# Relative attention: position tables inside the layernorm ahead, steps split last, first batch split by two engines

## What is computed

```python
Q, K, V = heads(x @ Wq.T + bq), heads(x @ Wk.T + bk), heads(x @ Wv.T + bv)   # 16 heads of 8
pos_key   = (rel_emb @ Wpk.T + bpk).reshape(128, 16, 8)
pos_query = (rel_emb @ Wpq.T + bpq).reshape(128, 16, 8)
scores = Q K^T * scale
scores += take(Q pos_key^T, clip(j - i + 64, 0, 127)) * scale
scores += take(K pos_query^T, clip(i - j + 64, 0, 127))^T * scale
out = softmax(scores) V @ Wo.T + bo
```

## Time and profile before

| what | us |
|---|---|
| median of three runs | 2801.14 (2800.57 to 2802.79) |
| the profiled execution | 2805.52 |
| its span | 2803.7 |
| TensorE busy | 2424.5 (86%) |
| VectorE busy | 2077.3 (74%) |
| ScalarE busy | 1585.5 (57%) |
| GpSimd busy | 269.5 (10%) |
| the layernorm ahead of the layer begins | 1457.0 |
| the layer's first instructions | 1471.1 |
| first band product | 1498.3 |
| first score product | 1519.1 |
| the next layernorm begins | 2026.4 |

### The profile page before, as it was taken

How to read it: one execution, slowest core, us unless ns; L and a number is a source line. 1 busy time by engine, 2 the same in 40 slices (tenths; PEclk the granted TensorE clock), 3 DMA queues, 4 the chain that set the end, 5 groups by cost and what they waited for, 6 DMA issues and landing times. The chain is left out here.

```text
span 2803.7 us, 64145 instructions
## 1 busy us (share of the span) xinstructions
PE 2424.5 (86%) x25861; PEld 1600.8 (57%) x25861; DVE 2077.3 (74%) x3811; ACT 1585.5 (57%) x4086; POOL 269.5 (10%) x278
## 2 busy tenths in 40 slices
PE   6888888888888888888994999999998887999777
PEld 5666676666666676674442666666642332332376
DVE  6899898899999989892124777788727775886465
ACT  3566666666667666665334777777641113667344
POOL 0000000000000000000011101100003342110342
PEclk9999999999999999999996999999999998999889
DMA  5111111110111111002007998999510003220421
GB/s 188 32 33 25 25 32 33 32 32 18 32 32 33 33 32 32 17 17 72 0 12 198 229 250 227 229 244 236 130 37 2 0 0 108 70 74 20 176 70 65
DMA packets 205727, 219.50 MB, mean 78 GB/s; under 512 B 32966, under 2 KB 191446, under 8 KB 199990
## 3 DMA queue, kind: packets, MB, share of 16 engines
q1 hardware_dynamic: 202400, 209.59, 28.5%
q0 software_dynamic: 2400, 4.95, 0.5%
q10 hardware_dynamic: 633, 0.85, 0.1%
HBM read 137.96 MB, written 79.79 MB: 78 GB/s over the span
## 5 line engine op out<-in xcount | busy, mean ns | idle before, releaser
L3003 DVE TENSOR_REDUCE dl_ZO<-dl_XP 128x64 f32<-128x128 f32 (+6 forms) x448 | 219.7, 491 | 15.4
L2116 ACT ACTIVATE da_AB<-ps 128x384 f32<-128x384 f32 x256 | 124.7, 491 | 137.7 <-PE ps L1963 134.1
L2578 PE MATMUL ps<-dl_ST,ident 128*128 128x512 f32 x416 | 187.8, 595 | 0.0
L2998 DVE TENSOR_TENSOR dl_XP<-dl_ZO,dl_G 128x128 f32<-128x128 f32 (+5 forms) x384 | 177.1, 461 | 13.2
L1596 DVE TENSOR_REDUCE ra_top<-ps 128x1 f32<-128x512 f32 x256 | 159.2, 680 | 36.1 <-PE ps L1362 35.2
L2126 ACT ACTIVATE da_E<-ps,da_top 128x512 f32<-128x512 f32 x256 | 176.2, 688 | 15.3 <-DVE da_top L2273 14.8
L2270 DVE TENSOR_TENSOR ps<-ps,da_window 128x192 f32<-128x192 f32 (+1 forms) x256 | 101.2, 395 | 111.5 <-PE ps L1986 107.2
L2273 DVE TENSOR_REDUCE da_top<-ps 128x1 f32<-128x512 f32 x256 | 177.0, 691 | 8.8
L1496 ACT ACTIVATE ra_PT<-ps 128x512 f32<-128x512 f32 x256 | 136.0, 601 | 61.0 <-PE ps L1393 60.7
L1993 PE MATMUL ps<-ident,da_E 128*128 128x128 f32 x1024 | 168.7, 288 | 1.3 <-ACT da_E L2126 1.3
L2512 PEld LDWEIGHTS ps<-X,dl_taps_v 128*128 128x128 f32 x1088 | 140.3, 210 | 16.6 <-issue 10.9
(11 more groups left out here) (416 smaller groups left out, 5932.2 us busy)
## 6 DMA issues: line engine op xcount, KB each, us to landing
da_bands<-da_AB SPq DMA_DIRECT2D x128, 384.0 KB, 3.8
dl_Abc<-dl_ends SPq DMA_DIRECT2D x64, 512.0 KB, 6.3
da_window<-da_bands SPq DMA_DIRECT2D x128, 192.0 KB, 4.4
da_across<-da_bands SPq DMA_DIRECT2D x128, 192.0 KB, 4.4
da_parts<-da_split SPq DMA_DIRECT2D x64, 96.0 KB, 3.4
ra_parts<-ra_split SPq DMA_DIRECT2D x16, 384.0 KB, 3.7
rf_We<-in_rf_We SPq DMA_DIRECT2D x1, 4608.0 KB, 22.8
da_K<-da_parts SPq DMA_DIRECT2D x16, 256.0 KB
```

The lines of the kernel that those rows point to most:

```text
L2116: eng.activation(AB[:, j % STAGES, h, :, :], ps[:, band_bank(v), 0:2 * BAND].rearrange("p (k x) -> p k x", k=2), ACT.Copy)\
L2578: eng.matmul(ps[:, UPDATES[r], :], c.ident[:, :], quarters[:, r, :, :], start=True, stop=alone)
L2998: link(eng.tensor_tensor(XP[:, :, :, SB - t:], seen.unsqueeze(1).to_broadcast([P, 2, I, t + 1]), G[:, x:x + 2, keys][:, ::-1, :].unsqueeze ...
L3003: link(eng.tensor_reduce(ZO[:, to:to + 1 + (2 * I - 1) * CH:CH].rearrange("p (k i) -> p k i", k=2), XP[:, :, :, SB - 1 - t:], AXX, ALU.add))
```

## The change

The tables are made in the layernorm: its hook `vector_blanks` gives way to `tensor_tables`, which replaces the five products of L113 and L114 by the two table products, four products of ones, the product of `chosen`, and four products of ones, and to `vector_tables`, called ahead of each of VectorE's four normalising products. VectorE's two blanks go: AT's to GpSimd, with the second half of the ones in QL, and QU's to VectorE in the layer behind the splits, under a semaphore of its own (`emptied`). ScalarE's blank of QL moves from the head of its list into `pack_tables`, and `pack_tables` ahead of the blanks of da_across. For all batches the three step instructions of GpSimd come behind the last parts of keys and queries, and the transfer of the steps behind those of the queries. For batch 0 VectorE makes the queries' subtraction and last part (counted by `halved`), and GpSimd passes the count on.

```diff
@@ -108,10 +109,14 @@
             mean_of(3)
             for b in range(1, B):
                 variance(b)
-            for b in range(B):
-                eng.wait_ge(centred, base + b + 1)
-                eng.matmul(c.ps[:, b, :], c.ones_mean[:, :], c.R[:, b, :], start=True, stop=True)
-            eng.matmul(c.ps[:, 0, :], c.ones_mean[:, :], c.R[:, 0, :], start=True, stop=True)
+            if tensor_tables:
+                eng.wait_ge(centred, base + B)
+                tensor_tables(eng)
+            else:
+                for b in range(B):
+                    eng.wait_ge(centred, base + b + 1)
+                    eng.matmul(c.ps[:, b, :], c.ones_mean[:, :], c.R[:, b, :], start=True, stop=True)
+                eng.matmul(c.ps[:, 0, :], c.ones_mean[:, :], c.R[:, 0, :], start=True, stop=True)
...
                 vector_blanks(eng)
             for b in range(B):
+                if vector_tables:
+                    vector_tables(eng, b)
                 eng.wait_ge(rstd, base + b + 1)
                 eng.wait_ge(centred, base + b + 1)
                 eng.tensor_tensor(c.X[:, b, PAD:PAD + T], D[:, b, :], Q[:, b, :], ALU.mult)
...
-    SELECTED = 10
-    JUMPED = SELECTED + 3
+    CHOSEN, SELECTED, JUMPED = 6, 11, 13
     TABLED = JUMPED + 4 + 4
-    CLEARED, BLANKED = 9, 2
+    CLEARED, BLANKED = 8, 2
+    QUERIES_SPLIT, KEYS_SPLIT = 4, 3
     CASTS, POOLED, SIDED, PROJECTED = 5, 7, 3, 4
     TABLE_PRODUCTS = 2
...
             half_ones(eng, 0)
-
-        def relative_vector_blanks(eng):
-            clear(eng, operand(QU, ROWS, P), 0.0)
+            eng.wait_ge(s["cleared"], 3)
             clear(eng, AT[ROWS:, :, :].rearrange("p h x -> p (h x)"), 0.0)
-
-        c.pool_blanks, c.vector_blanks = relative_pool_blanks, relative_vector_blanks
-        yield [(s["loaded"], pairs)]
+            eng.wait_ge(s["cleared"], 4)
+            half_ones(eng, 1)
+
...
+        def relative_tensor_tables(eng):
+            eng.wait_ge(s["loaded"], 16 * len(pairs))
+            eng.matmul(ps[:, 1, 0:P], Wp[:, 0, :], rel[:, 0, :], start=True, stop=True)
+            eng.matmul(ps[:, 1, P:2 * P], Wp[:, 1, :], rel[:, 1, :], start=True, stop=True).then_inc(s["projected"], 1)
+            for _ in range(4):
+                eng.matmul(ps[:, 3, :], c.ones_mean[:, :], c.R[:, 0, :], start=True, stop=True)
+            eng.wait_ge(s["tables"], CHOSEN)
+            eng.matmul(ps[0:HEADS, 2, 0:BAND], chosen[:, :], tables[:, 0, :], start=True, stop=True).then_inc(s["projected"], 1)
+            for _ in range(4):
+                eng.matmul(ps[:, 3, :], c.ones_mean[:, :], c.R[:, 0, :], start=True, stop=True)
+
+        def relative_vector_tables(eng, b):
+            def table(ins):
+                count[0] += 1
+                ins.then_inc(s["tables"], 1)
+
+            def settled():
+                eng.wait_ge(s["tables"], count[0])
+
+            pk, pq = pkq[:, 0, :], pkq[:, 1, :]
+            pk_low, pk_up, pq_low, pq_up = pk[:, 0:1], pk[:, P - 1:P], pq[:, P - 1:P], pq[:, 0:1]
+            if b == 0:
+                table(eng.memset(raised[:, :, :, :], 0.0))
+                table(eng.memset(jump[:, :], 0.0))
+                eng.wait_ge(s["loaded"], 16 * len(pairs))
+                eng.wait_ge(s["projected"], 1)
+                table(eng.tensor_tensor(pkq[:, :, :], ps[:, 1, 0:2 * P].rearrange("p (k x) -> p k x", k=2),
+                                        bias[:, PK:PQ + 1].unsqueeze(2).to_broadcast([P, 2, P]), ALU.add))
+                settled()
+            elif b == 1:
+                table(eng.tensor_scalar(chosen[:, :], heads[:, :], pq_low, -scale, ALU.mult, ALU.mult))
+                table(eng.tensor_scalar(A_table[:, 0:P], pk, pk_low, None, ALU.subtract))
+                table(eng.tensor_scalar(A_table[:, P:], pk_up.to_broadcast([P, BAND - P]), pk_low, None, ALU.subtract))
+                assert count[0] == CHOSEN, count
+                table(eng.tensor_tensor(ends[:, 0:1], bias[:, Wq:Wq + 1], pq_low, ALU.add))
+            elif b == 2:
+                table(eng.tensor_scalar(B_table[:, 0:SPAN + 1], pq_up.to_broadcast([P, SPAN + 1]), pq_low, scale, ALU.subtract, ALU.mult))
+                table(eng.tensor_scalar(B_table[:, SPAN + 1:], pq[:, 0:P - 1], pq_low, scale, ALU.subtract, ALU.mult))
+                settled()
+
+        c.pool_blanks, c.tensor_tables, c.vector_tables = relative_pool_blanks, relative_tensor_tables, relative_vector_tables
+        yield [(s["loaded"], pairs)]
...
         def projections(b, i):
-            return TABLE_PRODUCTS + PROJECTED * b + i if b else (2, 3, 5, 6)[i - 1]
+            return TABLE_PRODUCTS + PROJECTED * b + i
...
             def write_queries(m):
                 b, g = m // GROUPS, m % GROUPS
-                eng.wait_ge(s["pooled"], POOLED * (b + 1))
+                eng.wait_ge(s["pooled"], POOLED * b + QUERIES_SPLIT)
...
                 for part, first, times in REPEATED:
...
                     eng.dma_start(dst, split[rows, QUERIES, part, :].unsqueeze(1).to_broadcast([QUAD * DH, times, T])).then_inc(s["written"], 16)
+                if g == 0:
+                    eng.wait_ge(s["pooled"], POOLED * (b + 1))
+                    eng.dma_start(steps[b % 2], step_split[:, :, :]).then_inc(s["written"], 16)
 
             def write_keys(m):
                 b, g = m // GROUPS, m % GROUPS
-                eng.wait_ge(s["pooled"], POOLED * b + 6)
+                eng.wait_ge(s["pooled"], POOLED * b + KEYS_SPLIT)
...
                 for first, count in CYCLED:
...
                     eng.dma_start(dst, split[rows, KEYS, 0:count, :]).then_inc(s["written"], 16)
-                if g == 0:
-                    eng.dma_start(steps[b % 2], step_split[:, :, :]).then_inc(s["written"], 16)
...
             write_tables()
             write_keys(0)
             write_queries(0)
+            eng.wait_ge(s["emptied"], 1)
             pack(0)
             write_keys(1)
...
-            eng.wait_ge(s["loaded"], 16 * len(pairs))
-            eng.matmul(ps[:, 5, 0:P], Wp[:, 0, :], rel[:, 0, :], start=True, stop=True)
-            eng.matmul(ps[:, 5, P:2 * P], Wp[:, 1, :], rel[:, 1, :], start=True, stop=True).then_inc(s["projected"], 1)
             prepared(0, 0, Wq)
             prepared(0, 1, Wk)
-            eng.wait_ge(s["tables"], SELECTED)
-            eng.matmul(ps[0:HEADS, 6, 0:BAND], chosen[:, :], tables[:, 0, :], start=True, stop=True).then_inc(s["projected"], 1)
             steps_up(0)
             tokens(0)
             eng.wait_ge(s["loaded"], READY)
             eng.wait_ge(s["cleared"], CLEARED)
+            eng.wait_ge(s["emptied"], 1)
             for v in range(LEAD):
                 band(v)
             eng.wait_ge(s["blanked"], BLANKED)
...
+                zeros = c.X[ROWS:FIXED, 0, PAD + T:PAD + T + SPAN].unsqueeze(1).to_broadcast([FIXED - ROWS, GROUPS * QUAD * T // (2 * SPAN), SPAN])
+                eng.activation(operand(QL, ROWS, FIXED).bitcast(F32).rearrange("p (k x) -> p k x", x=SPAN), zeros, ACT.Copy).then_inc(s["cleared"], 1)
                 eng.wait_ge(s["cleared"], CLEARED)
+                eng.wait_ge(s["emptied"], 1)
                 src = bass.AP(fixed_parts.tensor, fixed_parts.offset, [[BAND, PARTS], [PARTS * BAND, HEADS], [1, BAND]])
                 eng.dma_start(AT[FIXED:FIXED + PARTS, :, :], src).then_inc(s["loaded"], 16)
                 eng.dma_start(QU[UPPER:UPPER + PARTS, :, :, :].rearrange("p g h t -> p (g h t)"),
...
-            zeros = c.X[ROWS:FIXED, 0, PAD + T:PAD + T + SPAN].unsqueeze(1).to_broadcast([FIXED - ROWS, GROUPS * QUAD * T // (2 * SPAN), SPAN])
-            eng.activation(operand(QL, ROWS, FIXED).bitcast(F32).rearrange("p (k x) -> p k x", x=SPAN), zeros, ACT.Copy).then_inc(s["cleared"], 1)
             for j in range(SIDES):
                 high(0, j)
             keep_steps(0)
             middle(0, KEYS, 1)
             middle(0, QUERIES, 2)
+            pack_tables()
             blank = c.X[:, 0, PAD + T:PAD + T + SPAN].unsqueeze(1).to_broadcast([P, RING * QUAD, SPAN])
             units = across[:, 0:RING * QUAD * WIDE].rearrange("p (u x) -> p u x", x=WIDE)
...
-            pack_tables()
             for v in range(LEAD):
...
             def prepare(b):
                 eng.wait_ge(s["projected"], projections(b, 3))
                 less(b, KEYS, 2)
-                less(b, QUERIES, 2)
+                if b:
+                    less(b, QUERIES, 2)
+                else:
+                    eng.wait_ge(s["pooled"], 1)
+                    eng.wait_ge(s["halved"], 1)
+                    eng.sem_inc(s["pooled"], 1)
+
+            def complete(b):
+                last(b, KEYS, 4)
+                if b:
+                    last(b, QUERIES, 5)
+                else:
+                    eng.wait_ge(s["pooled"], 3)
+                    eng.wait_ge(s["halved"], 2)
+                    eng.sem_inc(s["pooled"], 1)
                 eng.wait_ge(s["cast"], CASTS * b + 3)
```

(42 more changed lines are left out.)

20 lines of the change are left out of this document (2 added, 18 removed).

## The result

The changed kernel has a median of 2811.10 us over nine runs (2807.95 to 2819.3), the kernel before 2802.41 over nine. The ratio is 1.0039, with a 95% interval of 1.0027 to 1.0050. The prediction was 2812 (2807 to 2818), slower with a chance of 0.85. The profiled execution took 2815.92 us.

A forecast was written before the change was run, and what follows sets the result against it. In the steady relative attention TensorE was taken as the bound, stopped only by three 1.0 us waits for GpSimd's da_wide copy. Terms +9.1 + 3.8 - 1.3 = +11.6 on 2801.14 gave 2812 us, range 2807 to 2818.

The forecast's parts named there:

- Part 1, the steps last: Three batch handoffs: GpSimd's steps behind the last parts start TensorE's da_wide transposes 3.0 us later each, +9.1 us.
- the rival of an absorbed pause: At L2021, products behind `invert` would have waited anyway, so its 3.0 us delay costs nothing; 2800 us, chance 0.12.
- The clock: +3.8: Behind the three longer handoff pauses, TensorE's clock falls to half twice, at 1.9 us each; bounds 0 and 7.2.
- The rival that the clock holds: Behind the handoff pauses TensorE keeps full clock; 2809 us, chance 0.2.
- Part 2, the layernorm: Layernorm ahead of the layer: TensorE's added products and fillers start the layer 1.2 us later.
- The lock: Layernorm: VectorE's table operations wait behind GpSimd's memsets, TensorE ends 1.4 to 1.7 us later; 2814 us, chance 0.15.
- the sixth table step: VectorE's layernorm table work: under the lock, ready near 1469.4, not before the 1468.0 at which TensorE wants it.
- the 1469.3 of the working: Layernorm: when VectorE's normalising products would end, against 1470.85 before the change; no bound.
- Part 3, the first batch: Way into the layer: band copies start 0.8 to 1.9 us earlier, for a gain of -1.3 us.
- ScalarE's queue: Ahead of the first band copy: fixed-row wait, transfers and blanks end at 1496.9 to 1498.0, limiting the first batch's gain.
- 4.4 forecast: First batch: pack(0) on SP moves from 1493.33 to about 1489, so packed data are there 4.4 us earlier.
- The sum: The whole change: +9.1 + 3.8 - 1.3 = +11.6 us, added to the median of 2801.14.

The follow-up runs named there:

- order back: Changed kernel with GpSimd's steps ahead of the last parts again for batches 1 to 3, SP's waits to match: layer 567.28 us, ratio 1.0016.
- order alone: Kernel before with only the steps moved behind the last parts for batches 1 to 3, SP to match: layer 583.55 us, ratio 1.0060.
- the five traces: One profiled execution each of the five kernels, the changed one included, whose three waits for da_wide are 4.0 us: layers 581.23 to 583.55 us.
- e7_no_fillers: Changed kernel without the four products of ones behind the product of chosen, run once: layer 582.41 us.
- e10_memsets_later: Changed kernel with GpSimd's last two layernorm memsets held until VectorE's nine table operations are done, run once: layer 582.16 us.
- the seven traces: One trace each of four kernels with the changed start and three with the old: first handoff at 97.8 to 99.4 and 100.3 to 100.6 us.
- both repairs: Changed kernel with steps in their own tile, da_wide copy ahead of the last parts, ScalarE's old list: layer 563.24 and 563.29 us, ratios 0.9979 and 0.9983.
- the four kernels with the changed start: Changed kernel and three variants with the same instructions from the layernorm to the first handoff: first score at 60.7 to 61.2 us.
- the three with the old one: Kernel before and two variants of it that keep its start: first score at 62.0 to 63.0 us.
- the filled pause: Changed kernel with four unread products of 512 columns in TensorE's wait for da_wide at each handoff: layer 576.22 us, ratio 1.0029.

## Why the prediction was right, point by point

- **Part 1, the steps last: +9.1.** The subtractions, the two waits for ScalarE's casts, the steps and the copies came in the predicted order and spacing: the transposes 12.55 us behind the first subtraction, for 12.59 in the working. Waiting cost 8.7. The order back and the order alone show that this part carries the loss, and nothing absorbed it: the rival of an absorbed pause is out. This is the step that the prediction had fully right.
- **The clock: +3.8, measured 5.8.** The mechanism held; the size was low. I had two falls of three at 1.9. There were three, two at 1.4 and one at 3.0, because the half-clock stretch behind the third was twice as long. The rows at hand had low stretches of some 3 and of 4.7 us, and nothing in them tells which length follows a pause. The traces show that it changes from run to run, and with 8.7 of waiting taken off, the five traces put the term between 5.4 and 6.4. The rival that the clock holds is out for this kernel.
- **Part 2, the layernorm: 1.2 later, measured 1.3.** Ended by the fillers, as e7_no_fillers shows. The lock's mechanism was right in the rival and its price wrong: I let the sixth table step be ready behind GpSimd's last memset. VectorE got in between the two memsets, and the step was ready at 1464.1, ahead of the 1464.69 at which TensorE took it. The price of the lock lies on VectorE, which ended the layernorm 13.5 us from its start and not 12.2 (the 1469.3 of the working), and was no bound, as forecast. The rule of the Trainium skill that the prediction named ("SBUF — State Buffer", Who interferes with whom) holds here for memsets of GpSimd as well, by e10_memsets_later (1.1 to 1.5 us beside them, 0.23 to 0.28 without); the two fp32 products of X beside them stayed at 0.68 and 0.69.
- **Part 3, the first batch: -1.3, measured -0.8 to the first score and -2.5 to the first handoff.** ScalarE's queue was sized well: the fixed row left SP at 24.1 us from the start of the layernorm (23.1 to 24.2 forecast) and the first band copy came at 40.9 (39.8 to 40.9). SP issued the first packed tiles at 31.4 (31.9 forecast), and they were there 2.9 us earlier than before the change (2.7 to 4.5 over the seven traces) for 4.4 forecast; that does not matter while ScalarE's list ends later, and it is what limits both repairs. The 1.7 us between the first score and the first handoff are no gain that can be relied on: that stretch took 36.6 to 38.2 us in the four kernels with the changed start and 37.6 to 38.3 in the three with the old one. The longest wait of TensorE in it, 3.4 us after the change for 4.8 before, scatters as widely with the start unchanged (4.8 in the order back). The forecast of -1.3 lies inside what the seven traces give, -0.9 to -2.8.

The terms measured make -2.5 + 8.7 + 5.8 = 12.0, as the layer does; they must, since the legs of the order back are those of the kernel before. The sum had 11.6. That it came within 0.4 is partly luck: the clock was 2.0 short and the start's gain 1.2 short, and the two nearly cancel. In the total the ratio makes 2802.41 x 0.0039 = 10.9, and the medians differ by 8.7. Two slips of the working move nothing: 2812.7 was rounded to 2812 and not 2813, and a mean clock of 0.87 over 1542 to 1544 puts the return to full speed at 1542.5, not 1542.3.

## What to carry to other kernels

Before an engine's list is reordered so that one result comes sooner, look at what else is queued behind on that engine: here a half-microsecond copy for TensorE stood behind the moved work, and nothing in GpSimd's own times showed that it mattered; TensorE's wait list did. Ask also why the short urgent thing has to stand behind the long one: here it was only a shared tile, and a tile of 32 rows of its own removed it. And price a pause of TensorE above its length, at least if it grows from one to four microseconds in a dense stretch. Last, take a difference of one or two microseconds between single traces for a gain only when a third trace of the same stretch says how far it scatters.

## Not expected

- What the pauses grew by cost two thirds again in clock: 5.8 us behind 8.7 of added waiting. The half-clock stretch lasted some 3 us behind one pause of 3.98 us and some 6 behind another of the same length, in the same code, and the long one came behind the first, the second or the third wait depending on the trace.
- A pause of 2.42 us behind 5 us of dense fp32 products was enough for the fall (3.33 us for four passes that take 1.96 at full clock), while the filled pause with 0.56 us left kept 1.00.
- One-input operations of VectorE on 16 to 128 columns, 0.23 to 0.28 us alone, took 1.1 to 1.5 beside GpSimd memsets of 1.38 and 1.82 us. VectorE's own memset was not slowed: 3.47 us for 4096 columns with 1.80 us of a GpSimd memset beside it, 0.85 ns a column, and 1.34 for 1536 columns with none, 0.87.
